# One block for the recurrent, score and attention stages, and constant products in TensorE's holes

## The reference, cut to what matters

```python
x = x + L0(relu(layernorm(x)))     # graph products with the parts of adj
x = x + L1(relu(layernorm(x)))     # graph product, 128 -> 256 -> 128, two batchnorms
x = x + L2(relu(layernorm(x)))     # two graph products, then four LSTMs over windows of
                                   # 1, 2, 3 and 4 consecutive nodes; each writes its last node
x = x + L3(relu(layernorm(x)))     # attention over 256 edges (src, dst), 4 heads
# L3:
Xq, Xv = H @ W_lin.T, H @ W_val.T
e = sum_d(leaky_relu(Xq[src] + Xq[dst], 0.2) * a) + log(adj[src, dst] + 1e-8)
attn = exp(e - segment_max(e, src)) / segment_sum(exp(...), src)
Y = segment_sum(attn * Xv[dst], src); out = Y @ W_out.T
```

## Time and profile before

| | |
|---|---|
| median of 3 runs | 1319.07 us (1316.67 to 1319.22) |
| the profiled execution | 1317.13 us, of which the span is 1315.4 us |
| PE busy | 1214.1 us, 92% |
| DVE busy | 1018.3 us, 77% |
| ACT busy | 898.0 us, 68% |
| POOL busy | 325.0 us, 25% |
| mean granted TensorE clock | 0.967 of full |
| moved by DMA | 37.90 MB |

### The profile page before, as it was taken

One profiled execution on the slowest core, in us unless ns is written; L12 is line 12 of the kernel. 1 busy time (PEld: TensorE's weight loads), 2 busy tenths in 40 slices (PEclk: granted clock), 3 DMA queues, 4 the chain that ended last, 5 costly groups with the idle time before them and its releaser, 6 DMA issues. The chain is left out here.

```text
span 1315.4 us, 23598 instructions
## 1 busy us (share of the span) xinstructions
PE 1214.1 (92%) x6996; PEld 994.1 (76%) x6996; DVE 1018.3 (77%) x2037; ACT 898.0 (68%) x1681; POOL 325.0 (25%) x738
## 2 busy tenths in 40 slices
PE   2999988979979998899999999999998899978998
PEld 1989985643358886689879888987886677747998
DVE  4787766996768885988788879887775699976664
ACT  1766647857758886877687778777765799842332
POOL 3576750000057440000000000000000566633331
PEclk8999998998969999999999999999999799998999
DMA  7000000000031110000000000003000200000112
GB/s 298 1 0 0 0 0 0 0 0 0 0 137 64 64 57 1 0 1 1 1 0 1 0 1 1 1 1 128 1 1 33 97 0 1 1 0 33 73 73 81
DMA packets 14467, 37.90 MB, mean 29 GB/s; under 512 B 1856, under 2 KB 3904, under 8 KB 13120
## 3 DMA queue, kind: packets, MB, share of 16 engines
q1 hardware_dynamic: 13008, 36.31, 7.1%
q10 hardware_dynamic: 1392, 0.74, 0.2%
HBM read 20.27 MB, written 16.78 MB: 28 GB/s over the span
## 5 line engine op out<-in xcount | busy, mean ns | idle before, releaser
L955 ACT ACTIVATE gates<-bank,lstm_bias 128x512 f32<-128x512 f32 (+1 forms) x504 | 301.5, 636 | 101.5 <-PE bank L944 88.3
L139 ACT ACTIVATE l_h<-X,nmr,rstd 128x128 f32 (+1 forms) x512 | 210.1, 484 | 54.2 <-POOLq L133 32.8
L929 PE MATMUL bank<-lstm_node_hi,Wih_hi 128*128 128x512 f32 (+1 forms) x408 | 149.4, 366 | 0.0
L931 PE MATMUL bank<-lstm_node_lo,Wih_hi 128*128 128x512 f32 (+1 forms) x408 | 148.9, 365 | 0.0
L930 PE MATMUL bank<-lstm_node_hi,Wih_lo 128*128 128x512 f32 (+1 forms) x408 | 148.8, 365 | 0.0
L108 POOL TENSOR_TENSOR l2r_sum<-l2r_st 128x8 f32<-128x8 f32 x16 | 3.3, 208 | 532.2 <-DVE l2r_st L89 531.9
L940 PE MATMUL bank<-lstm_hid_hi,Whh_hi 128*128 128x512 f32 (+1 forms) x288 | 104.2, 362 | 4.5 <-DVE lstm_hid_hi L1011 4.3
L944 PE MATMUL bank<-lstm_hid_lo,Whh_hi 128*128 128x512 f32 (+1 forms) x288 | 106.8, 371 | 0.0
L941 PE MATMUL bank<-lstm_hid_hi,Whh_lo 128*128 128x512 f32 (+1 forms) x288 | 103.1, 358 | 0.0
L960 ACT ACTIVATE gates<-lstm_cell 128x512 f32<-128x512 f32 (+1 forms) x144 | 83.7, 581 | 21.6 <-DVE lstm_cell L998 21.3
L931 PEld LDWEIGHTS bank<-lstm_node_lo,Wih_hi 128*128 128x128 f32 x408 | 77.1, 189 | 11.7
(11 more groups left out here) (245 smaller groups left out, 3258.5 us busy)
## 6 DMA issues: line engine op xcount, KB each, us to landing
X<-in_x SPq DMA_DIRECT2D x8, 1024.0 KB, 14.1
x_spill<-X SPq DMA_DIRECT2D x32, 256.0 KB, 2.0
X<-x_spill SPq DMA_DIRECT2D x2, 4096.0 KB, 12.4
out<-X SPq DMA_DIRECT2D x32, 256.0 KB, 2.0
w_raw<-in_WihT SPq DMA_DIRECT2D x1, 1024.0 KB, 5.9
w_raw<-in_WhhT SPq DMA_DIRECT2D x1, 1024.0 KB, 8.1
W<-in_L_W ACTq DMA_DIRECT2D x1, 192.0 KB, 5.2
rows<-in_rows ACTq DMA_DIRECT2D x1, 128.0 KB, 4.4
```

The costliest lines, as they stand in the source:

```text
L139: last = act.activation(h[:, j, :], k.X[:, bass.ds(b0, TB), :][:, j, :], ACT.Relu, bias=k.nmr[:, bass.ds(b0, TB)][:, j:j + 1], scale=k.rst ...
L929: pe.matmul(out, hi, x_high, start=True, stop=False)
L931: last = pe.matmul(out, hi, x_low, start=False, stop=it.step == 0)
L955: act.activation(gate_of(it, g), k.bank[4 * s + g][:, 0:it.N], ACT.Tanh if g == GATE_G else ACT.Sigmoid, bias=k.lstm_bias[:, it.p - 1, g:g ...
```

## The change

The three last stages become one block: `stage_lstm_to_attend`, with classes `Scores` and `Attend` whose tiles lie at fixed places over the recurrent stage's buffers and weights. The barrier and the semaphore clearing are gone. The first residual update, its statistics and the first normalisation stand among the last instructions of the recurrent stage. `Residual.fetch` is gone: PE transposes straight out of `HT`. All turns are written out without `Fori`. Chunk 0's softmax and the gathers and weightings of tiles 0 and 1 stand in turns 14 and 15 of the scores; `linear_term` and `turn_in` work on one chunk at a time. `stay_awake` issues products of constants on PE whose result nobody reads, in the stages before too: 26 at the end of `stage_layer0`, 8 and 12 at the ends of `stage_gcn_hidden`, 16 and 6 in `stage_gcn_out`, 8 and a list by tile (`FILL`) in `stage_conv`, 28 behind the recurrent stage.

```diff
+def stay_awake(pe, k, bank, n):
+    for _ in range(n):
+        pe.matmul(bank[:, 0:P], k.ident[:, :], k.ones[:, :], start=True, stop=True)
...
+    FILL = {-4: 8, -3: 6, -2: 10, -1: 10, 0: 10, 1: 8, 2: 6, 3: 4}
...
                     res.turn_over(pe, turn, s)
+                stay_awake(pe, k, k.bank[7], FILL.get(t, 0) if isinstance(t, int) else 0)
...
 # stage_lstm -> stage_lstm_to_attend, SyncE
+            for s in range(S):
+                sp.wait_ge(computed[s], ends[s].n + 1)
+            sp.dma_start(k.X[:, head:, :], k.x_spill[:, head:, :]).then_inc(x_tail, 16)
...
 # TensorE
+                if it is items[-1]:
+                    pe.wait_ge(act_out[0], gate_count(ends[0], GATE_O))
+                    for r in range(sc.S):
+                        sc.turn_over(pe, 0, r)
...
+            stay_awake(pe, k, k.bank[3], 28)
+            pe.wait_ge(act_out[1], gate_count(ends[1], GATE_O))
+            sc.on_tensor(pe, at)
+            at.on_tensor(pe)
...
 # ScalarE
+            sc.normalise(act, 0, 0)
             tanh_of_cell(before)
+            sc.normalise(act, 0, 1)
...
 # VectorE, ahead of new_cell(it)
+                if it is items[-1]:
+                    dve.wait_ge(x_head, 16)
+                    sc.update(dve, 0, x_tail)
...
+class Scores:
+    def turn_over(self, pe, i, s):
+        if i:
+            pe.wait_ge(self.R["updated"][s], i)
+        for j in range(TB):
+            b = (i * self.S + s) * TB + j
+            last = pe.transpose(self.psR[s][:, j * P:(j + 1) * P], self.states[:, b // GROUP, :, b % GROUP], self.k.ident[:, :])
+        last.then_inc(self.R["R"][s], 1)
...
+    def on_scalar(self, act, at):
...
+            if i == n_it - 2:
+                for t in range(2):
+                    at.high(act, t)
+                at.sm.exponential(act, 0)
...
+    def on_tensor(self, pe, at):
...
+            if i == n_it - 2:
                 for s in range(S):
+                    pe.wait_ge(R["updated"][s], n_it)
+                at.sm.linear_term(pe, 0)
+            if i == n_it - 1:
+                at.sm.turn_back(pe, 0)
...
+            if i == n_it - 2:
+                at.sm.turn_in(pe, 0)
+            if i == n_it - 1:
+                at.sm.sum_up(pe, 0)
             for s in range(S):
+                if i == n_it - 1 and s == S - 1:
+                    at.gather(pe, 0)
...
+        pe.wait_ge(R["M"][0], n_it)
+        at.gather(pe, 1)
...
+    def on_vector(self, dve, tail_in, at):
...
+            if i + AHEAD < n_it:
+                self.update(dve, i + AHEAD, tail_in)
+            if i == n_it - 2:
+                at.sm.add_linear(dve, 0)
+            if i == n_it - 1:
+                at.sm.keep_exponential(dve, 0)
+                at.sm.invert(dve, 0)
+                at.sm.weigh(dve, 0)
...
+            if i == n_it - 2:
+                at.sm.score_in(dve, 0)
+                at.sm.max_forward(dve, 0)
+                at.sm.max_backward(dve, 0)
+                at.sm.subtract_max(dve, 0)
+            if i == n_it - 1:
+                for t in range(2):
+                    at.weighted(dve, t)
 # then the two reductions of scores and the two of q_sums, as before
...
+class Attend: # steps are range(-2, tiles + 1)
+    def on_tensor(self, pe):
+        for t in self.steps:
+            if there(t):
+                self.scatter(pe, t)
+            if there(t + 2) and t + 2 > 1:
+                self.gather(pe, t + 2)
+            if due(t, 10):
+                sm.linear_term(pe, due(t, 10))
+            if due(t, 9):
+                sm.turn_in(pe, due(t, 9))
...
+    def on_vector(self, dve):
...
+            if due(t, 10):
+                sm.add_linear(dve, due(t, 10))
+            if due(t, 9):
+                sm.score_in(dve, due(t, 9))
+                sm.max_forward(dve, due(t, 9))
```

More of the change, by code:

```diff
@@ L897, in x_halves @@
         return [columns(it, part[it.tile % 2][it.slot]) for part in (x_hi, x_lo)]
+    ends = [[it for it in items if it.slot == s][-1] for s in range(S)]
     with nc.Block() as block:
@@ L1035, in _ @@
             new_hidden(before)
+            sc.on_vector(dve, x_tail, at)
+            at.on_vector(dve)
 def stage_edges(k, ctx, e):
@@ L1357, in turn_in, with halves, linear_term @@
-    def turn_in(self, pe, q):
-        pe.wait_ge(self.summed, self.EC)
-        for c in range(self.EC):
-            last = pe.transpose(self.ps_in[q][:, c * P:(c + 1) * P], self.scores[:, c, q * P:(q + 1) * P], self.k.ident[:, :])
+    def halves(self, place):
+        return place.rearrange("p (c x) -> p c x", c=self.EC)
+    def linear_term(self, pe, q):
+        if q:
+            pe.wait_ge(self.inverted, q)
+        for c in range(self.EC):
+            last = pe.matmul(self.first[:, c * P:(c + 1) * P], self.e.PT[:, c * P:(c + 1) * P],
+                             self.e.q_sums[:, q * P:(q + 1) * P], start=True, stop=True)
+        last.then_inc(self.linear, 1)
@@ L1361, in turn_in, with add_linear @@
+    def add_linear(self, dve, q):
+        dve.wait_ge(self.linear, q + 1)
+        dve.scalar_tensor_tensor(self.chunk(q), self.halves(self.first), 0.25, self.chunk(q),
+                                 ALU.mult, ALU.add).then_inc(self.summed, 1)
+    def turn_in(self, pe, q):
+        pe.wait_ge(self.summed, q + 1)
+        for c in range(self.EC):
+            last = pe.transpose(self.second[:, c * P:(c + 1) * P], self.scores[:, c, q * P:(q + 1) * P], self.k.ident[:, :])
         last.then_inc(self.turned, 1)
@@ L1399, in sum_up @@
             for n in range(self.EC):
-                last = pe.matmul(self.place(1)[:, c * P:(c + 1) * P], self.e.same[:, n, c * P:(c + 1) * P],
+                last = pe.matmul(self.second[:, c * P:(c + 1) * P], self.e.same[:, n, c * P:(c + 1) * P],
                                  self.scores[:, n, q * P:(q + 1) * P], start=n == 0, stop=n == self.EC - 1)
@@ L1432, in stage_attend @@
-    tiles = k.B // TB
-    psV, psY, psO = (k.bank[0:2], k.bank[2:4]), (k.bank[4], k.bank[6]), k.bank[7]
-    E = k.E
-    sm = Softmax(k, ctx, attn, e, [ps[:, n * E:(n + 1) * E] for ps in (psY[1], psO) for n in range(2)], k.bank[5])
-    PER_CHUNK = tiles // sm.NQ
-    as_tile = lambda ps: ps[:, :].rearrange("p (b n) -> p b n", b=TB)
-    tile_of = lambda buf, t: buf[:, t * TB:(t + 1) * TB, :]
-    there = lambda t: 0 <= t < tiles
-    FIRST, LAST = -3, tiles + 1
-    def due(t, ahead):
-        q, left = divmod(t + ahead, PER_CHUNK)
-        return q if left == 0 and 0 < q < sm.NQ else None
@@ new lines, in value_tile, with gather @@
+    def value_tile(self, t):
+        return self.Xv[:, t * TB:(t + 1) * TB, :]
+    def gather(self, pe, t):
+        self.wait(pe, self.vlo_done, t)
+        self.wait(pe, self.Vw_done, t, 2)
+        for c in range(self.k.E // P):
+            for part in (self.v_hi, self.v_lo):
+                last = pe.matmul(self.psV[t % 2][c][:, :], self.e.DTr[:, c * P:(c + 1) * P], part[t % 2][:, :, :],
+                                 start=part is self.v_hi, stop=part is self.v_lo)
+        last.then_inc(self.V_done, 1)
@@ new lines, in scatter, with project @@
+    def scatter(self, pe, t):
+        self.wait(pe, self.Vw_done, t)
+        self.wait(pe, self.YT_done, t, 2)
+        EC = self.k.E // P
+        for j in range(TB):
+            for c in range(EC):
+                last = pe.matmul(self.psY[t % 2][:, j * P:(j + 1) * P], self.Vw[t % self.W][:, c, j, :],
+                                 self.e.S1[:, c, :].bitcast(F32), start=c == 0, stop=c == EC - 1)
+        last.then_inc(self.Yp_done, 1)
+    def project(self, pe, t):
+        self.wait(pe, self.YT_done, t)
+        self.wait(pe, self.added, t, 1)
+        for j in range(TB):
+            last = pe.matmul(self.psO[:, j * P:(j + 1) * P], self.YT[t % 2][:, j, :], self.e.WoT[:, :], start=True, stop=True)
+        last.then_inc(self.O_done, 1)
@@ new lines, in on_scalar @@
+    def on_scalar(self, act):
+        there, due, sm = self.there, self.due, self.sm
+        for t in self.steps:
+            if there(t + 3) and t + 3 > 1:
+                self.high(act, t + 3)
+            if there(t):
+                self.wait(act, self.Yp_done, t)
+                self.wait(act, self.O_done, t, 2)
+                act.activation(self.YT[t % 2][:, :, :], as_tile(self.psY[t % 2]), ACT.Copy).then_inc(self.YT_done, 1)
+            if due(t, 6):
+                sm.exponential(act, due(t, 6))
@@ new lines, in on_pool @@
+    def on_pool(self, pool):
+        for t in range(2, self.tiles):
+            self.low(pool, t)
+    def on_vector(self, dve):
+        there, due, sm, X = self.there, self.due, self.sm, self.k.X
+        for t in self.steps:
+            if there(t + 2) and t + 2 > 1:
+                self.weighted(dve, t + 2)
+            if there(t - 1):
+                self.wait(dve, self.O_done, t - 1)
+                xt = X[:, (t - 1) * TB:t * TB, :]
+                dve.tensor_tensor(xt, as_tile(self.psO), xt, ALU.add).then_inc(self.added, 1)
```

(17 more changed lines are left out.)

514 lines of the change are left out of this document (212 added, 302 removed).

## The result

The changed kernel takes **1303.55 us** (median of 4 runs, 1302.56 to 1304.55) against 1317.87 (4 runs, 1316.66 to 1319.22) for the kernel before beside it: a ratio of 0.9891, 95% interval 0.9874 to 0.9908. I had forecast 1314, in a range of 1301 to 1321. The direction and the range hold; the size is that of my first rival, 1305. The profiled execution took 1302.56 us, its span 1300.8, which is 14.6 under that of before.

A forecast was written before the change was run, and what follows sets the result against it. PE, busy 92% of the span, was taken as the bound, with DVE 0.16 us from it in the score loop. 7.8 - 9.0 + 4.5 - 1.3 + 2.4 = 4.4 us gain; forecast 1314 us, range 1301 to 1321.

The forecast's parts named there:

- first rival: Score turns: PE reads HT at full speed, so no 9.0 us loss and DVE stays the bound; 1305 us, chance 0.35.
- the forecast's own case: Whole kernel: the forecast's terms hold, with the time at 1310 to 1319 us by the joins' bounds; chance 0.47.
- Transposes straight from HT: Score turns: strided weight loads cost PE 0.11 us more each, turn 9.6 us against DVE's 8.91; loss 9.0 us.
- DVE and PE both bound this loop: Steady score turn: DVE's work fills 8.91 us and PE needs 8.75 without a hole, 0.16 us apart.
- ACT was not the bound: nothing: Score turns: removing ACT's gathers (2 x 1.08 us) from every turn gains nothing.
- Join before the scores: Recurrent stage to scores: barrier, ACT's gathers ahead of the first transposes and cold PE go; gain 7.8 us, bounds 5 and 10.5.
- Join before the attention: Scores' last turns to first scatter: softmax work moves earlier, scatter 0 at 1186.5 against 1191.03; gain 4.5 us, bounds 2 and 12.
- Chunks 2 and 3: Attention stage: each brings 0.67 us of PE work, a linear term and a turn, into a full stretch; loss 1.3 us.
- Constants in earlier stages: Holes after layer 0, before 297.79 and in stage_conv: constant products keep PE's clock up; 1.3 + 2.0 - 0.9, gain 2.4 us.
- slower strided loads: Score turns: strided loads cost four times a load's time, PE's turn 11.4 us; 1337 us, chance 0.06.
- constants in the way: stage_conv: fillers run at half clock, 44 cost 20 us instead of 10 and hold PE up; 1324 us, chance 0.04.
- the join that gives nothing: Before the scores: ACT's wait ahead of the last tanh holds things up as long as the barrier did; 1322 us, chance 0.08.

The follow-up runs named there:

- contig: Changed kernel with PE's transposes of the recurrent states reading contiguous floats in place of floats 64 bytes apart: 1301.97 us, ratio 0.9879.
- doubled: Changed kernel with every PE transpose out of HT done twice into the same place: 1314.25 us, ratio 0.9975.
- two fetch runs: Changed kernel with ACT's gathers out of HT put back, unread, behind each normalise (1307.56 us) or where the kernel before had them (1303.66 us).
- fetch_in_place: Changed kernel with ACT's two gathers of HT put back between the copies of h and of the queries, turns 1 to 12, unread: 1303.66 us.
- tanh_first: Changed kernel with ACT's last tanh of the recurrent stage ahead of the first normalise: 1301.05 us, ratio 0.9883.
- together: Changed kernel with reordered joins, earlier value halves, spread reductions, later chunk 1 to 3 steps, 24 join constants and none in stage_conv: 1288.48 us, ratio 0.9783.
- nofill: Changed kernel with no constant products at all: 1306.71 us, ratio 0.9918.
- noconv: Changed kernel without the constant products of stage_conv (the 8 ahead of its loop and FILL): 1302.13 us, ratio 0.9880.
- four single edits: Changed kernel, each alone: exponential and turn_back later 1301.84 us; last tanh before normalise 1301.05; value halves earlier 1300.27; chunk 1 to 3 steps later 1299.39.
- straight_alone: Kernel before with only PE transposing straight out of HT and ACT's gathers gone, other engines keeping their loops: 1312.14 us, ratio 0.9965.

## Why the prediction was right and wrong

The time fell inside 1301 to 1321 because that range took in the first rival's 1305; within the forecast's own case it had ended at 1310. So the hit on the range says nothing for the mechanism, whose largest term was wrong.

**The step that failed is "Transposes straight from HT", the loss of 9.0.** It carried ACT's price for a 64-byte step, 0.11 us for 128 floats, over to TensorE's weight loads. Measured: 0.004 us a load (contig: 8.76 against 8.785 us a turn) and 0.113 for a whole transpose (doubled), where I had 0.22. I had named ACT's row as the nearest and chose it over the row nearer in kind, TensorE's own transposes, which showed the distance from one to the next but nothing of what a load needs of it. With the 9.0 at nothing the sum would have been 1304 beside the profile's 1302.6, and the rival that said so had only 0.35. I had named a turn of 8.9 as what refutes the step; it came out as 8.785. The ACT figure itself was sound: 1.06 to 1.10 us for 512 such floats came back in the two fetch runs (medians 1.07 and 1.08).

On ACT, where the 64-byte step costs 0.9 ns a float, and on TensorE, where it costs 0.03 ns, the same memory was read. The Trainium skill's rule on 16-byte lines (Advanced Engine Details and Errata, SBUF Cachelines) names no engine; here ACT's row agrees with it and the time of TensorE's turn doesn't; of TensorE only the longer record of the load (194 ns, not 142) does. The Trainium skill's other rule, that a load's time goes by its column count (TensorE: Matmul & The Clock Gate, Step-by-step: what each phase is for), is the one that the turn's time agrees with, in that the step adds next to nothing; loads of other column counts weren't tried.

**"DVE and PE both bound this loop" and "ACT was not the bound: nothing" failed too**, by 1.6 us to the good side. In the earlier trace rows VectorE's work fills the turn, but its relus hold short waits for PE's edge sums, and those waited for queries that stood in ACT's queue behind two gathers: eight of them take 3.76 us in the fetch_in_place run and 3.60 in the changed kernel. With the gathers gone the turn fell from 8.92 to 8.785, with them back in place it was 8.93. ACT's queue set the turn. I had gone by ACT's share of the whole span, 68%, where the loop has its own: in 1050 to 1140 us ACT was busy 82.28 of 90 us before, 91%, and 66.16 after (columns as in the earlier trace rows, first the kernel before).

```profile
1050.00:1140.00 90.00, 90.00 (x569) 67.89 (x568) 88.11 (x182) 82.28 (x162) 58.79 (x121) 1.00 0.00 0
1050.00:1140.00 90.00, 90.00 (x581) 70.38 (x581) 89.03 (x185) 66.16 (x145) 59.58 (x122) 1.00 0.00 1
```

And the 8.75 us that I took from the earlier trace rows as what PE needs in a steady turn are those of turn 13, the first behind ACT's last gather (1140.2 in the earlier trace rows). The turn before it took 8.92 with the same instructions on PE. The gain stood in the rows and I read it as slack of PE.

**Join before the scores, 7.8 forecast: 6.8.** The first score transpose came 7.7 us earlier by itself (10.7 less the 2.95 of the stages before), against 7.1. The second turn was 1.0 later than said. The order was as I described it: the last tanh behind the normalise, then the hidden state, then update 1. The term that was too small is "POOL's coefficients take 4.2": they took 5.5, from 1009.62 to 1015.1.

```profile
1009.62 1.09 POOL L119 TENSOR_TENSOR l2r_sum<-l2r_st 128x8 f32<-128x8 f32 x1 [522.77 <-DVE l2r_st L100]
...
1010.84 0.65 POOL L119 TENSOR_TENSOR l2r_m<-l2r_st 128x8 f32<-128x8 f32 x1
```

These two take 0.21 us each in the kernel before and in the second turn; here they stand beside VectorE's three cell operations (1009.36 to 1011.42), which the barrier had kept apart from them. So the normalise came 1.5 us later than the forecast less 2.95 has it, and the second turn's statistics reached GpSimd at 1021.1 and not at 1020.0. The tanh_first run put 2.3 us on the order of tanh and normalise, which I had bounded at "3 more, or nothing".

**Join before the attention, 4.5 forecast: 4.5**, and each part where it was said: the exponential's hole in turn 15 (3 said, 3.7 seen), half clock behind it (1.7 said, 1.3 seen), `turn_in` ahead of scatter 0 (6 said, 5.6 seen) and a scatter at half clock. Not seen by me: the first scan takes 1.79 us beside GpSimd's subtractions, which made the hole 1.1 longer. My upper bound for this gain was 12, "if scatter 0 didn't wait behind `turn_in`". That was for this kernel's order. With all three places mended, in the together run, scatter 0 comes 22.0 us behind turn 14's transposes, 36.1 in the kernel before: 14.1.

**Chunks 2 and 3, loss 1.3: 1.4**, from the second scatter to the last addition (115.8 to 117.2 us). No run took this term apart.

**Constants in earlier stages, gain 2.4: 2.95.** The hidden stage gave 1.5 (1.3 said), less 0.2 by which its first product waited for the constants; the out stage 2.5 (2.0 said), `stage_conv` lost 0.85 (0.9 said). The nofill and noconv runs turn these differences on and off: 4.7 and 1.0.

Of the rivals, slower strided loads are out by contig and doubled, constants in the way by nofill and noconv, and the join that gives nothing by the 6.8 us that it gave.

## What to carry to other kernels

A price belongs to the engine that pays it: before a row of ACT is carried over to a weight load, look whether the load shows in the engine's time at all, and give the rival that it doesn't at least an even chance. Read an engine's busy share in the loop in question and not over the whole span, and read what stands in its queue ahead of the instruction that others wait for: an engine with 68% on the page, 91% in the loop and no idle time ahead of that instruction set this loop's turn. When a wait is removed from one place in a chain, the next instruction in the same queues decides: here four single edits gave 1.0, 2.3, 2.4 and 4.4 us inside their stages, 10.1 in sum, and the kernel with all of them and some more was 15.1 us faster as a whole. One of the four, alone, had only moved its hole.

## What the runs showed of the hardware

- TensorE loads 128 x 128 float32 weights from 64-byte steps at the rate of contiguous ones (0.113 and 0.109 us from one transpose to the next) although the records of the loads are 194 and 142 ns long. Why a longer load doesn't show is open; other steps were not tried.
- VectorE's scan over 256 columns took 1.79 us beside GpSimd's subtractions of 128 x 512 and 0.69 without them. The addition of 128 x 256 right ahead of it, beside the same subtractions, took its usual 0.41. A scan of `max_backward` in the changed kernel's attention stage took 1.25 with a subtraction beside part of it. `weigh`, a product of two 128 x 256 tiles in SBUF, took 1.47 in the kernel before (1188.18, beside a subtraction that ended at 1189.37) and 0.42 in the changed one, with none beside it. The scan reads two tiles from SBUF, the addition one from SBUF and one from PSUM. The Trainium skill (SBUF — State Buffer, SBUF: two separate sides) says that a VectorE operation with two SBUF inputs and a GpSimd operation that reads SBUF take turns on one port pair, the later one waiting for the whole of the other. The trace agrees: the second subtraction ends at 1154.67, and a scan of 0.69 that began only then would end within 0.2 us of the 1155.22 seen. The rows fit it the other way round too: two of GpSimd's 128 x 8 instructions, 0.21 us each elsewhere, took 1.09 and 0.65 beside VectorE's cell operations, which read two tiles from SBUF. That they waited for a port is argued from these times; no run took it apart.
- The same hole doesn't always cost the same. In the second turn PE idles 1.82 us in the changed kernel and goes on at full clock (edge sums 1.98 us); it idled 1.89 in the contig run and the next ones took 3.04. Behind equal holes of 3.66 us the half clock lasted about a microsecond longer in the kernel before than in straight_alone. An estimate of what a hole costs in clock is uncertain by as much: 1.0 us in this pair, 1.7 in the first, whose second turns start 12.6 and 10.9 us behind the first ones.
- The 8, 44 and 18 products of constants kept the granted clock at full through `stage_conv` and lost 1.0 us: PE was busy 13.9 of 23 us there without them, and the other engines waited little for it. Where PE fed the others at once, behind the two earlier holes, such products gave 4.7.
